# Key and query biases added in PSUM by a product, and elu+1 as one exponential and one min/max

## The chip, the cores and the metric

The kernel runs on one core of a Trainium2 chip. The metric is device time in microseconds (us), the median of several timed runs. A core has five engines that run side by side and wait for each other by semaphores: TensorE (PE in the rows; its weight loads are PEld), VectorE (DVE), ScalarE (ACT), GpSimd (POOL) and SyncE (SP, which here only issues transfers). TensorE writes its results into PSUM, a small memory of banks of 128 partitions x 512 fp32; VectorE and ScalarE read PSUM and SBUF, the main on-chip memory.

## The reference, cut to what matters

`x` and `ctx_1024` are (32, 128, 128): 32 sequences of 128 tokens of width 128. A layer of causal linear attention with 16 heads of width 8, then a layer of 8 experts of which each token takes two:

```
q  = layernorm(x) @ Wq + bq          # per token, 128 wide
k  = ctx @ Wk + bk
v  = ctx @ Wv + bv
qp = elu(q) + 1                      # = max(q + 1, min(exp(q), 1))
kp = elu(k) + 1
out[t] = sum over s <= t of (kp[s] . qp[t]) v[s]   per head
out    = (out / cumsum(qp)) @ Wo + bo
x = x + out
x = x + moe(layernorm(x))            # router, top 2 of 8, gated ffn
```

The biases are not zero: `bk` is drawn with a spread of 0.608, `bq` with 0.1.

## The kernel before, in words

The 32 sequences are worked in 8 units of 4 sequences, 512 tokens each. A unit's projections, scores and values are tiles of 128 partitions x 512. The code of every engine is written out by hand in the order in which it is to run, with waits on counting semaphores; `body(u, par)` of an engine is what it does while unit `u`'s attention runs. The units are overlapped: in `body(u)` the engines also do the *front* of unit `u + 1` (normalise, transpose and project x, project the context, elu+1, spread the keys and values) and the *tail* of unit `u - 1` (output projection, second layernorm, router, ranks). So `body(1)` to `body(6)` hold the fronts of units 2 to 7, and what precedes `body(0)` holds the front of unit 0.

The part that the change touches, in the front of unit `u + 1`:

- TensorE projects the keys into PSUM bank 1 (`front_project_k`, L1360), after VectorE has emptied the bank (`vexp_done`), and the queries into bank 0 (`front_project_q`, L1364), after ScalarE has copied the transposed x (`xT_copied`). The biases are not in these products.
- ScalarE computes elu+1's exponential in two steps: `front_neg` (L780) writes Relu(-(p + b)) from the bank p to `expn`, and `front_exp` (L785) overwrites it with Exp(-that), which is min(exp(p + b), 1). Index m is 0 for keys, 1 for queries.
- VectorE ends with one operation (`elu_k` L1000, `elu_q` L1004): max((p + (b + 1)), expn), the bank as its first tensor, b + 1 as a per-partition scalar.

In ScalarE's body the key's pair stands ahead of `front_norm` (L757, four operations, x normalised) and of `off_scores(u, 1)` (L817, scores copied from PSUM to `Pm`). VectorE's `mask_scores(u, 1)` (L1041) waits for that copy, and `front_z`, `weights` and `mask_scores(u, 2)` stand behind it. The query's Relu stands behind `off_scores(u, 2)`; then `tail_x2` (L822, the copy of the transposed second layernorm), and then the query's Exp.

TensorE's body holds the key projection ahead of `scores(u, 1)`, and the query projection between `scores(u, 2)` and the transposes of `tail_x2` (L1430). Products with a matrix of zeros (L1460) stand between them in the bodies 1 to 6.

The output bias and the router's bias are already added in PSUM in this way: GpSimd splits them into three bf16 parts that sum to the fp32 value (`biases`, L712 to L720, nine operations after `body(0)`'s own), puts these in rows 0, 32 and 64 of `bias_rows` with zeros between, and TensorE multiplies by a matrix of ones in bf16 (L1420, L1435), ahead of the fp32 products into the same bank.

After the attention a table of tiles is made and the experts run (L1552 to L1581). Its first tile waits until GpSimd has scattered the rows of units 0 to 5 to memory (L617, paced through the bodies, then without a pause) and SyncE has loaded the tile.

At the start SyncE issues the loads in a fixed order: x and context of unit 0, the weights Wk and Wq (`qk_pack`), Wv, Wo and others (`vo_pack`), three pieces of expert weights, then x and context of unit 1. VectorE takes the statistics of unit 1's x ahead of unit 0's `elu_k`.

Of the kernel before, what the change touches and what calls it, by code (L numbers as in the profile page):

```python
# [6 lines left out]
ALU = mybir.AluOpType  # L7
# [8 lines left out]
P = 128  # L16
# [5 lines left out]

def attention_moe_kernel(nc, x_tok, ctx_t, qk_pack, vo_pack, w_pack, out_tok):
    L, NB, D = x_tok.shape
# [3 lines left out]
    UB = 4  # L28
# [34 lines left out]
    with ExitStack() as ctx:  # L63
# [17 lines left out]
        carrier = sb("carrier", [P, 5])  # L81
        BIAS = P + 2 * E
# [4 lines left out]
        vo_s = sb("vo_s", [P, 4 * P + 3 * E])  # L87
        Wv_s, Wo_s, bv_b, _ = (vo_s[:, k * P:(k + 1) * P] for k in range(4))
        confT, _, wealth_b = (vo_s[:, 4 * P + k * E:4 * P + (k + 1) * E] for k in range(3))
        bq_neg, bk_neg = sb("bq_neg", [P, 1]), sb("bk_neg", [P, 1])  # L90
# [125 lines left out]
        exp_warm = sb("exp_warm", [P, 1])  # L216
        hid = sb("hid", [P, 2, HC * TT])
        hid_hi = sb("hid_hi", [P, 2, 2, HC * TT], F16)

# [39 lines left out]
        qk_loaded = sem("qk_loaded")  # L259
        const_loaded = sem("const_loaded")  # L260
        const_made = sem("const_made")
        const_dve = sem("const_dve")
# [101 lines left out]
        ROUTER = 8  # L364
        N_BIAS = 9
        N_EARLY = 13
        N_MADE = 35

# [72 lines left out]
        def _(sp):  # L441
# [23 lines left out]
            for m in range(3):  # L465
                load_w(0, m)
            load_x(1)
            load_ctx(1)
# [103 lines left out]
        def _(pool):  # L572
# [114 lines left out]
            made(pool.memset(seg_cols[:, E - 1:E], float(-(E - 1) * 3 * I)))  # L687
            made(pool.memset(cols_at[:, 0:1], 0))
            made(pool.memset(before[:], 0.0))
            made(pool.memset(unit_ids[:], TOP * UT))  # L690
# [11 lines left out]
            def biases():  # L702
# [10 lines left out]
                part(pool.tensor_copy(bias_part[0], given))  # L713
                part(pool.tensor_copy(bias_rows[0:1, :], bias_part[0][0:1, :]))
                part(pool.tensor_tensor(bias_rest, given, bias_part[0], ALU.subtract))
                part(pool.tensor_copy(bias_part[1], bias_rest))
# [32 lines left out]
        def _(act):  # L749
# [98 lines left out]
            def body(u, par):  # L848
# [115 lines left out]
        def _(dve):  # L964
# [33 lines left out]
            def elu_k(u, par):  # L998
                dve.wait_ge(exp_done, 2 * u + 1)
                dve.scalar_tensor_tensor(kT[:], bank[1][:], bk_one[:], expn[:, 0, :], ALU.add, ALU.max).then_inc(qk_done, 1)  # L1000

            def elu_q(u, par):
                dve.wait_ge(exp_done, 2 * u + 2)
                dve.scalar_tensor_tensor(qT[par][:], bank[0][:], bq_one[:], expn[:, 1, :], ALU.add, ALU.max).then_inc(qk_done, 1)  # L1004

# [340 lines left out]
        def _(pe):  # L1346
            def front_transpose_x(u):
# [17 lines left out]

# [49 lines left out]
            def tail_out(u):  # L1415
                if not first(u):
                    pe.wait_ge(rows_to_done, u)
                if first(u):
                    pe.wait_ge(bias_made, N_BIAS)
                pe.matmul(tail_bank(u).rearrange("p (b d) -> p b d", b=UB), ones_b[:], bias_rows[:, 0:P].unsqueeze(1).to_broadcast([P, UB, P]),  # L1420
                          start=True, stop=False, skip_group_check=True)
# [11 lines left out]
            def tail_logits(u):  # L1433
                pe.wait_ge(x2T_copied, u + 1)
                pe.matmul(tail_bank(u)[:, 0:UB * E].rearrange("p (b e) -> p b e", b=UB), ones_b[:], bias_rows[:, P + E:BIAS].unsqueeze(1).to_broadcast([P, UB, E]),  # L1435
                          start=True, stop=False, skip_group_check=True)
# [240 lines left out]
```

## Time and profile before

| | us |
|---|---|
| median of 3 timed runs | 344.05 |
| lowest and highest of them | 343.34, 345.0 |
| span of the profiled execution (first to last instruction) | 343.3 |
| TensorE busy | 296.6 (86%) |
| VectorE busy | 271.9 (79%) |
| ScalarE busy | 234.0 (68%) |
| GpSimd busy | 194.4 (57%) |

The profiled execution has no time of its own beside its span; the span lies 0.04 us below the lowest timed run and 0.75 us below the median. A busy share is an average over stages with different limits: the attention units and the experts' tiles each take about half of the span. To read a stage, look for the engine that never waits there, and for the one wait that it has.

### The profile page before, as it was taken

To read this page: it belongs to the slowest core of one execution; us is meant where nothing else is said; L and a number is where in the kernel's file an instruction comes from. 1 tells how busy PE (TensorE), PEld (TensorE's weight loads), DVE (VectorE), ACT (ScalarE), POOL (GpSimd) and SP (SyncE) were. 2 spreads that over 40 slices of the span, in tenths; PEclk is the share of its full clock that TensorE was granted. 3 is DMA by queue.
4 is the path that set the end of the run, shared out by engine and by line. 5 is a ranking of instruction groups with operands and counts; after the bars stand their busy time and mean duration, and the time that the engine had idled before them with its cause. 6 is when DMAs were issued, how large, how long until landed. Compare 5 with 4: busy or idle time off the path is not lost.

```text
span 343.3 us, 12426 instructions
## 1 busy us (share of the span) xinstructions
PE 296.6 (86%) x4520; PEld 241.5 (70%) x4520; DVE 271.9 (79%) x749; ACT 234.0 (68%) x480; POOL 194.4 (57%) x303
## 2 busy tenths in 40 slices
PE   7588888979888898978789989999999979799970
PEld 5367575746657575664568979989899969699930
DVE  6679898999999899999868697996678745567681
ACT  3587886959778795961747867767677756577720
POOL 6800306676677767587578757777455554245440
PEclk9789999999999999989989999999999999999996
DMA  7032322415233331320144314576799653432968
GB/s 246 18 94 63 95 63 60 128 33 143 77 103 104 100 103 34 84 90 33 35 91 87 73 41 75 149 127 181 232 202 256 198 156 41 70 71 63 290 185 301
DMA packets 50026, 39.45 MB, mean 115 GB/s; under 512 B 32806, under 2 KB 39340, under 8 KB 49968
## 3 DMA queue, kind: packets, MB, share of 16 engines
q1 hardware_dynamic: 44784, 28.63, 31.7%
q0 software_dynamic: 4320, 8.47, 8.7%
q10 hardware_dynamic: 864, 1.57, 1.2%
q8 instruction: 38, 0.62, 0.8%
q14 instruction: 20, 0.16, 0.2%
HBM read 15.16 MB, written 12.21 MB: 80 GB/s over the span
## 4 chain that ended last, share of the span: by engine, by line
PE 40%; DVE 28%; issue 9%; DMA 8%; ACT 7%; POOL 6%; SPq 1%; POOLq 0%; ACTq 0%; DVEq 0%
DVE Pm L1041 6%; PE bank L1552 4%; PE bank L1554 4%; PE bank L1553 4%; POOL by_expert L617 4%; PE scores L1554 4%; PE scores L1552 4%; PE scores L1553 4%; PE bank L1581 4%; PE bank L1573 4%; PE bank L1574 4%; DVE w_lo L1106 3%; DVE Vexp L1013 3%; PE bank L1360 3%; DMA xgT<-by_expert 2%
## 5 line engine op out<-in xcount | busy, mean ns | idle before, releaser
L617 POOL DMA_INDIRECT by_expert<-token_rows,rows_to x64 | 65.7, 1026 | 27.9 <-issue 18.9
L737 POOL DMA_INDIRECT by_token<-y_sb,row_meta x55 | 56.4, 1025 | 43.9 <-ACT y_sb L906 31.7
L1294 DVE SCALAR_TENSOR_TENSOR hid<-scores,silu 128x512 f32<-128x512 f32 x71 | 48.4, 690 | 34.6 <-PE scores L1554 29.2
L915 ACT ACTIVATE silu<-bank 128x512 f32<-128x512 f32 x71 | 42.0, 596 | 27.1 <-PE bank L1554 24.2
L922 ACT ACTIVATE hid_hi<-hid 128x512 f16<-128x512 f32 x71 | 44.4, 628 | 19.5 <-DVE hid L1294 18.5
L1300 DVE TENSOR_TENSOR Kexp<-hid,hid_hi 128x512 f16<-128x512 f32 x71 | 50.0, 715 | 9.0 <-ACT hid_hi L922 6.3
L1389 PEld LDWEIGHTS scores<-qT,Kexp 32*128 32x128 f32 x1024 | 33.1, 194 | 20.9 <-DVE Pm L1041 16.0
L1041 DVE TENSOR_TENSOR Pm<-scores,causal 128x512 f32<-128x512 f32 x64 | 41.1, 685 | 7.0 <-ACT Pm L817 6.5
L1389 PE MATMUL scores<-qT,Kexp 32*128 32x128 f32 (+1 forms) x1024 | 37.6, 285 | 9.9 <-DVE Pm L1041 6.7
L817 ACT ACTIVATE Pm<-scores 128x512 f32<-128x512 f32 x32 | 18.8, 588 | 24.3 <-PE scores L1389 24.2
L1574 PE MATMUL bank<-w_lo,hid_hi 128*128 x248 | 34.3, 219 | 0.0
L1573 PE MATMUL bank<-w_hi,hid_hi 128*128 x248 | 34.3, 219 | 0.0
L1405 PE MATMUL bank<-Pm,Vexp 128*32 128x64 f32 (+1 forms) x1024 | 27.9, 250 | 7.2 <-DVE Pm L1041 7.2
L1552 PE MATMUL bank<-xgT,w_hi 128*128 128x256 f16 x96 | 26.7, 278 | 4.5 <-DMA xgT<-by_expert 2.5
L1405 PEld LDWEIGHTS bank<-Pm,Vexp 128*32 128x32 f32 x1024 | 22.7, 110 | 11.1 <-DVE Pm L1041 8.1
L1554 PE MATMUL bank<-xgT,w_lo 128*128 128x256 f16 x96 | 26.7, 278 | 0.0
L1553 PE MATMUL bank<-xgT,w_hi 128*128 128x256 f16 x96 | 26.6, 277 | 0.0
L1552 PE MATMUL scores<-xgT,w_hi 128*128 128x256 f16 x96 | 26.5, 276 | 0.0
L584 POOL TENSOR_TENSOR nm<-zero,mv 128x4 f32<-128x4 f32 x16 | 3.2, 202 | 41.1 <-DVE mv L971 41.0
L1553 PE MATMUL scores<-xgT,w_hi 128*128 128x256 f16 x96 | 26.5, 276 | 0.0
L1554 PE MATMUL scores<-xgT,w_lo 128*128 128x256 f16 x96 | 26.5, 276 | 0.0
L1574 PEld LDWEIGHTS bank<-w_lo,hid_hi 128*128 128x128 f16 x248 | 24.3, 98 | 0.3
(392 smaller groups left out, 793.5 us busy)
## 6 DMA issues: line engine op xcount, KB each, us to landing
w_raw<-in_w_pack_dram SPq DMA_DIRECT2D x24, 256.0 KB, 3.0
x_all<-in_x_tok_dram SPq DMA_DIRECT2D x8, 256.0 KB, 3.3
cT<-in_ctx_t_dram SPq DMA_DIRECT2D x8, 256.0 KB, 3.0
out_dram<-x_all ACTq DMA_DIRECT2D x6, 256.0 KB, 5.0
by_expert<-pad_row SPq DMA_DIRECT2D x9, 130.0 KB
by_expert<-token_rows,rows_to POOLq DMA_INDIRECT x64
token_rows<-by_token SPq DMA_DIRECT2D x2, 512.0 KB, 4.8
by_token<-y_sb,row_meta POOLq DMA_INDIRECT x55
```

The lines of the kernel that those rows point to most:

```text
L617: pool.indirect_dma_start(by_expert, bass.IndirectOffsetOnAxis(ap=rows_to[u % 2][:, s, b:b + 1], axis=0), token_rows[u % 2][:, b, s, :], N ...
L737: pool.indirect_dma_start(by_token, bass.IndirectOffsetOnAxis(ap=number, axis=0), y_sb[:, k, s, :], None, bounds_check=NT * TOP - 1, oob_i ...
L1041: dve.tensor_tensor(Pm[:, b % 2, :, at:at + CH].rearrange("p (r j) t -> p r j t", r=RG), score_groups[:, :, :, at:at + CH], causal[:].unsq ...
L1294: dve.scalar_tensor_tensor(hid[:, slot, :], bank[2 + slot], 1.0 / WSCALE, silu[:, slot, :], ALU.mult, ALU.mult).then_inc(hid_done, 1)
L1300: dve.tensor_tensor(hid_lo[:, k % 2, slot, :], hid[:, slot, :], hid_hi[:, k % 2, slot, :], ALU.subtract).then_inc(lo_done, 1)
L1389: ins = pe.matmul(scores4[:, r, j * SPAN + at:j * SPAN + at + n], Kexp[par][rows, c, 2 * j:2 * j + 2, :], qT[par][rows, c * CH:c * CH + n] ...
L1405: ins = pe.matmul(bank[6][32 * r:32 * r + 32, c * CH:c * CH + n], Vexp[par][:, c, 2 * r:2 * r + 2, :].rearrange("p g k -> p (g k)")[:, 16 ...
L1552: pe.matmul(ps, high, x_hi, start=(c == 0), stop=False, skip_group_check=True)
L1553: pe.matmul(ps, high, x_lo, start=False, stop=False, skip_group_check=True)
L1554: ins = pe.matmul(ps, low, x_hi, start=False, stop=True, skip_group_check=True)
L1573: pe.matmul(ps, hid_hi[:, k % 2, slot, h], high, start=(c == 0 and s == 0), stop=False, skip_group_check=True)
L1574: pe.matmul(ps, hid_hi[:, k % 2, slot, h], low, start=False, stop=False, skip_group_check=True)
```

## The change: what it does

From unit 2 on (`PLAIN = 2`) a bf16 product, `lift`, writes b + 1 into the bank ahead of the projection, which then accumulates on it: the bank holds p + b + 1. ScalarE's exponential reads the bank itself, Exp(bank - 1) with the -1 from a one-column tile `minus_one`, and there is no Relu. VectorE's operation becomes max(min(expn, 1), bank): the bank is now its second tensor, and its scalar is the constant 1. Units 0 and 1 keep the old form.

For this the key and query biases go, raised by 1, through the same split as the other two: `bias_rows` grows from 144 to 392 columns and GpSimd's work on it from nine operations to ten. The biases come in a transfer of their own, `bias_pack`, that lands in `hid` (the experts' tile, unused by then); `vo_pack` loses the columns that held the two old ones.

```
@@ sync
             for m in range(3):
                 load_w(0, m)
+            sp.dma_start(bias_given, bias_pack).then_inc(bias_loaded, 16)
             load_x(1)
             load_ctx(1)
@@ gpsimd
+            made(pool.memset(minus_one[:], -1.0))
...
-                pool.wait_ge(const_loaded, 16)
-                given = vo_s[:, 3 * P:3 * P + BIAS]
+                pool.wait_ge(bias_loaded, 16)
+                lifted = bias_given[:, 0:QK].rearrange("p (m d) -> p m d", m=2)
+                part(pool.tensor_tensor(lifted, lifted, ones[:].unsqueeze(1).to_broadcast([P, 2, P]), ALU.add))
                 part(pool.memset(bias_rows[:], 0.0))
@@ scalar
-                act.wait_ge(neg_done, 2 * u + m + 1)
-                act.activation(expn[:, m, :], expn[:, m, :], ACT.Exp, scale=-1.0).then_inc(exp_done, 1)
+                if u < PLAIN:
+                    act.wait_ge(neg_done, 2 * u + m + 1)
+                    act.activation(expn[:, m, :], expn[:, m, :], ACT.Exp, scale=-1.0).then_inc(exp_done, 1)
+                else:
+                    if u == PLAIN:
+                        act.wait_ge(const_made, N_MADE)
+                    ps, ready = ((bank[1], k_ps), (bank[0], q_ps))[m]
+                    act.wait_ge(ready, u + 1)
+                    act.activation(expn[:, m, :], ps[:], ACT.Exp, bias=minus_one[:]).then_inc(exp_done, 1)
...
-                    front_neg(u + 1, 0)
+                    if u + 1 < PLAIN:
+                        front_neg(u + 1, 0)
                     front_exp(u + 1, 0)
                     front_norm(u + 1)
...
-                if not last(u):
+                if u + 1 < PLAIN:
                     front_neg(u + 1, 1)
@@ vector, from unit 2 on (elu_q likewise with bank[0] and qT)
-                dve.scalar_tensor_tensor(kT[:], bank[1][:], bk_one[:], expn[:, 0, :], ALU.add, ALU.max).then_inc(qk_done, 1)
+                    dve.scalar_tensor_tensor(kT[:], expn[:, 0, :], 1.0, bank[1][:], ALU.min, ALU.max).then_inc(qk_done, 1)
@@ tensor
+            def lift(ps, m):
+                pe.wait_ge(bias_made, N_BIAS)
+                pe.matmul(ps.rearrange("p (b t) -> p b t", b=UB), bias_rows[:, m * P:(m + 1) * P], ones_b[:].unsqueeze(1).to_broadcast([P, UB, P]),
+                          start=True, stop=False, skip_group_check=True)
...
+                if u >= PLAIN:
+                    lift(bank[1], 0)
-                pe.matmul(bank[1], Wk_s, cT[par][:], start=True, stop=True).then_inc(k_ps, 1)
+                pe.matmul(bank[1], Wk_s, cT[par][:], start=(u < PLAIN), stop=True, skip_group_check=True).then_inc(k_ps, 1)
...
                 pe.wait_ge(xT_copied, u + 1)
-                pe.matmul(bank[0], Wq_s, xT[:], start=True, stop=True).then_inc(q_ps, 1)
+                if u >= PLAIN:
+                    lift(bank[0], 1)
+                pe.matmul(bank[0], Wq_s, xT[:], start=(u < PLAIN), stop=True, skip_group_check=True).then_inc(q_ps, 1)
```

How this stands in the engines' queues, at the places where another engine waits. A row is one instruction, or several alike, with its line in its own kernel, what it writes and reads, and the semaphores that it waits for. First ScalarE in the body of a unit from 2 on, from the last copy of the expert weights (`w_hi`) to the scores' copy for which VectorE waits. Before:

```order
L753 ACTIVATE w_hi<-w_raw 128x512 [waits w_loaded0_2]
L780 ACTIVATE expn<-bank,bk_neg 128x512 [waits k_ps]
L785 ACTIVATE expn<-expn 128x512 [waits neg_done]
L757 ACTIVATE xhat<-x_all,shift,rstd 128x128 [waits xT_ps,shift1_done]
L757 ACTIVATE xhat<-x_all,shift,rstd 128x128 x3
L817 ACTIVATE Pm<-scores 128x8x64 [waits av_done,scores_ps]
```

Now:

```order
L761 ACTIVATE w_hi<-w_raw 128x512 [waits w_loaded0_2]
L800 ACTIVATE expn<-bank,minus_one 128x512 [waits k_ps]
L765 ACTIVATE xhat<-x_all,shift,rstd 128x128 [waits xT_ps,shift1_done]
L765 ACTIVATE xhat<-x_all,shift,rstd 128x128 x3
L832 ACTIVATE Pm<-scores 128x8x64 [waits av_done,scores_ps]
```

The Relu is gone, and the exponential that stood behind it waits for the key projection itself (`k_ps`).

ScalarE again, later in the same body, from the second layernorm (`x2hat`) and the third copy of scores to the query's exponential. Before:

```order
L757 ACTIVATE x2hat<-x_all,shift,rstd 128x128 x3
L817 ACTIVATE Pm<-scores 128x8x64 [waits av_done,scores_ps]
L780 ACTIVATE expn<-bank,bq_neg 128x512 [waits q_ps]
L822 ACTIVATE x2T<-bank 128x512 [waits x2T_ps]
L785 ACTIVATE expn<-expn 128x512 [waits neg_done]
```

Now:

```order
L765 ACTIVATE x2hat<-x_all,shift,rstd 128x128 x3
L832 ACTIVATE Pm<-scores 128x8x64 [waits av_done,scores_ps]
L837 ACTIVATE x2T<-bank 128x512 [waits x2T_ps]
L800 ACTIVATE expn<-bank,minus_one 128x512 [waits q_ps]
L818 ACTIVATE zinv<-Z,seed_bias 128x512 [waits rz_done,z_done]
```

The query's Relu is gone from between the copy of scores and the copy of the transposed layernorm (`x2T`), and the exponential keeps its place behind that copy.

TensorE around the key projection of `body(1)`, behind the zero products. Before:

```order
L1460 MATMUL bank<-ones_b,zero_b 128x512 x4
L1360 MATMUL bank<-cT,qk_s 128x512 [waits vexp_done]
L1389 MATMUL scores<-qT,Kexp 128x128 [waits diag_done]
L1389 MATMUL scores<-qT,Kexp 128x128 x3
L1389 MATMUL scores<-qT,Kexp 128x64 x4
```

Now:

```order
L1492 MATMUL bank<-ones_b,zero_b 128x512 x4
L1380 MATMUL bank<-ones_b,bias_rows 128x512 [waits bias_made,vexp_done]
L1390 MATMUL bank<-cT,qk_s 128x512
L1421 MATMUL scores<-qT,Kexp 128x128 [waits diag_done]
L1421 MATMUL scores<-qT,Kexp 128x128 x3
L1421 MATMUL scores<-qT,Kexp 128x64 x4
```

The bias product takes over the wait for VectorE's emptying of the bank and stands, with a wait on GpSimd's bias work, ahead of the projection.

SyncE at the start, from the load of `vo_pack` to that of unit 1's context. Before:

```order
L464 DMA vo_s<-in_vo_pack_dram 128x536
L459 DMA w_raw<-in_w_pack_dram 128x512 x3
L446 DMA x_all<-in_x_tok_dram 128x512
L453 DMA cT<-in_ctx_t_dram 128x512
L453 DMA cT<-in_ctx_t_dram 128x512 [waits k_ps,v_ps]
```

Now:

```order
L469 DMA vo_s<-in_vo_pack_dram 128x400
L464 DMA w_raw<-in_w_pack_dram 128x512 x3
L472 DMA hid<-in_bias_pack_dram 128x392
L451 DMA x_all<-in_x_tok_dram 128x512
L458 DMA cT<-in_ctx_t_dram 128x512
L458 DMA cT<-in_ctx_t_dram 128x512 [waits k_ps,v_ps]
```

The bias load stands ahead of unit 1's x and context, and the load of `vo_s` is 136 columns narrower.

## Rows read from the trace of the kernel before

**Rows 1.** Top line of the page: the span of the profiled execution.

```profile
span 343.3 us, 12426 instructions
```

**Rows 2.** Waits of VectorE, 34 to 150 us: total us, times, longest us.

```profile
DVE Pm L1041 <- ACT Pm L817: 4.4, 6, 0.7
```

**Rows 3.** Chain of waits, unit 4: start us, duration us, engine, tile, line.

```profile
94.94 1.14 PE bank L1360 x2
96.10 0.70 ACT expn L780
```

**Rows 4.** ScalarE, unit 4: start, busy us, engine, line, operation, tiles, shapes, count.

```profile
96.82 0.63 ACT L785 ACTIVATE expn<-expn 128x512 f32<-128x512 f32 x1
97.36 1.63 ACT L757 ACTIVATE xhat<-x_all,shift,rstd 128x128 f32<-128x128 f32 x4
103.10 0.68 ACT L780 ACTIVATE expn<-bank,bq_neg 128x512 f32<-128x512 f32 x1
103.67 0.59 ACT L822 ACTIVATE x2T<-bank 128x512 f32<-128x512 f32 x1
104.15 0.63 ACT L785 ACTIVATE expn<-expn 128x512 f32<-128x512 f32 x1
```

**Rows 5.** VectorE, unit 4; in brackets the idle us before and its releaser.

```profile
98.05 0.72 DVE L1000 SCALAR_TENSOR_TENSOR kT<-bank,bk_one,expn 128x512 f32<-128x512 f32 x1
99.51 1.29 DVE L1041 TENSOR_TENSOR Pm<-scores,causal 128x512 f32<-128x512 f32 x2 [0.74 <-ACT Pm L817]
104.97 0.74 DVE L1004 SCALAR_TENSOR_TENSOR qT<-bank,bq_one,expn 128x512 f32<-128x512 f32 x1
```

**Rows 6.** Bias products: TensorE timeline, chain, then weight loads (PEld).

```profile
32.85 0.39 PE L1420 MATMUL bank<-bias_rows,ones_b 128*128 128x512 bf16 x1
...
177.74 0.22 PE scores L1420
...
91.84 0.10 PEld L1420 LDWEIGHTS bank<-bias_rows,ones_b 128*128 128x128 bf16 x1 [0.28 <-DVE rows_to L1100]
94.94 0.30 PEld L1360 LDWEIGHTS bank<-cT,qk_s 128*128 128x128 f32 x2 [0.97 <-DVE Vexp L1013]
```

**Rows 7.** TensorE, unit 4: query projection and the transposes behind it.

```profile
101.90 1.12 PE L1364 MATMUL bank<-xT,qk_s 128*128 128x512 f32 x2
102.86 0.60 PE L1430 MATMUL bank<-ident,x2hat 128*128 128x128 f32 x4
```

**Rows 8.** Page, costliest groups: busy us, mean ns, idle before.

```profile
L1294 DVE SCALAR_TENSOR_TENSOR hid<-scores,silu 128x512 f32<-128x512 f32 x71 | 48.4, 690 | 34.6 <-PE scores L1554 29.2
```

**Rows 9.** Chain, start; then a window: engines busy, PEclk, DMA share, GB/s.

```profile
4.08 5.90 DMA x_all<-in_x_tok_dram
...
7.50:8.00 0.50, 0.50 (x20) 0.50 (x22) 0.50 (x1) 0.50 (x2) 0.43 (x2) 1.00 1.02 385
```

**Rows 10.** GpSimd's bias work, first and last of nine; VectorE's first scans.

```profile
14.12 0.22 POOL L712 MEMSET bias_rows<- 128x144 bf16 x1
17.31 0.30 POOL L720 COPY bias_rows<-xgT 1x144 bf16<-1x144 bf16 x1
...
23.43 1.36 DVE L1021 TENSOR_TENSOR_SCAN Z<-ones,qT 128x128 f32<-128x128 f32 x4
```

**Rows 11.** One VectorE line twice; GpSimd beside the second.

```profile
149.71 0.71 DVE L1034 SCALAR_TENSOR_TENSOR Z<-zser_oT,zinv 128x512 f32<-128x512 f32 x1
...
170.98 1.68 DVE L1034 SCALAR_TENSOR_TENSOR Z<-zser_oT,zinv 128x512 f32<-128x512 f32 x1
...
170.95 2.72 POOL L603 TENSOR_TENSOR token_rows<-x2hat,token_rows 128x512 f16<-128x512 f32 x2 [3.12 <-ACT token_rows L829]
```

**Rows 12.** GpSimd in unit 6; chain at the first expert tile's load.

```profile
143.09 1.21 POOL L617 DMA_INDIRECT by_expert<-token_rows,rows_to  x1 [1.86 <-ACT Pm L817]
...
170.35 2.81 DMA xgT<-by_expert
```

**Rows 13.** Window, start of the experts' stage; PEclk stands third from the right.

```profile
175.00:176.00 1.00, 1.00 (x7) 0.69 (x6) 0.12 (x1) 0.12 (x1) 0.89 (x1) 0.50 0.31 30
```

More of the change, by code:

```diff
@@ L20, with attention_moe_kernel @@
 SEED_BIAS = -129.0 * math.log(2.0) - 0.0299
-def attention_moe_kernel(nc, x_tok, ctx_t, qk_pack, vo_pack, w_pack, out_tok):
+def attention_moe_kernel(nc, x_tok, ctx_t, qk_pack, vo_pack, bias_pack, w_pack, out_tok):
     L, NB, D = x_tok.shape
@@ L81, in attention_moe_kernel @@
         carrier = sb("carrier", [P, 5])
-        BIAS = P + 2 * E
+        QK = 2 * P
+        BIAS = QK + P + E
         bias_rows = sb("bias_rows", [P, BIAS], BF16)
@@ L86, in attention_moe_kernel @@
         Wk_s, Wq_s, bk_c, bq_c = qk_s[:, 0:P], qk_s[:, P:2 * P], qk_s[:, 2 * P:2 * P + 1], qk_s[:, 2 * P + 1:2 * P + 2]
-        vo_s = sb("vo_s", [P, 4 * P + 3 * E])
-        Wv_s, Wo_s, bv_b, _ = (vo_s[:, k * P:(k + 1) * P] for k in range(4))
-        confT, _, wealth_b = (vo_s[:, 4 * P + k * E:4 * P + (k + 1) * E] for k in range(3))
+        vo_s = sb("vo_s", [P, 3 * P + 2 * E])
+        Wv_s, Wo_s, bv_b = (vo_s[:, k * P:(k + 1) * P] for k in range(3))
+        confT, wealth_b = (vo_s[:, 3 * P + k * E:3 * P + (k + 1) * E] for k in range(2))
+        minus_one = sb("minus_one", [P, 1])
         bq_neg, bk_neg = sb("bq_neg", [P, 1]), sb("bk_neg", [P, 1])
@@ L217, in attention_moe_kernel @@
         hid = sb("hid", [P, 2, HC * TT])
+        bias_given = hid[:, 0, 0:BIAS]
         hid_hi = sb("hid_hi", [P, 2, 2, HC * TT], F16)
@@ L260, in attention_moe_kernel @@
         const_loaded = sem("const_loaded")
+        bias_loaded = sem("bias_loaded")
         const_made = sem("const_made")
@@ L364, in attention_moe_kernel @@
         ROUTER = 8
-        N_BIAS = 9
+        N_BIAS = 10
+        PLAIN = 2
         N_EARLY = 13
-        N_MADE = 35
+        N_MADE = 36
         def units(engine, body):
@@ L999, in elu_k @@
                 dve.wait_ge(exp_done, 2 * u + 1)
-                dve.scalar_tensor_tensor(kT[:], bank[1][:], bk_one[:], expn[:, 0, :], ALU.add, ALU.max).then_inc(qk_done, 1)
+                if u < PLAIN:
+                    dve.scalar_tensor_tensor(kT[:], bank[1][:], bk_one[:], expn[:, 0, :], ALU.add, ALU.max).then_inc(qk_done, 1)
+                else:
+                    dve.scalar_tensor_tensor(kT[:], expn[:, 0, :], 1.0, bank[1][:], ALU.min, ALU.max).then_inc(qk_done, 1)
             def elu_q(u, par):
                 dve.wait_ge(exp_done, 2 * u + 2)
-                dve.scalar_tensor_tensor(qT[par][:], bank[0][:], bq_one[:], expn[:, 1, :], ALU.add, ALU.max).then_inc(qk_done, 1)
+                if u < PLAIN:
+                    dve.scalar_tensor_tensor(qT[par][:], bank[0][:], bq_one[:], expn[:, 1, :], ALU.add, ALU.max).then_inc(qk_done, 1)
+                else:
+                    dve.scalar_tensor_tensor(qT[par][:], expn[:, 1, :], 1.0, bank[0][:], ALU.min, ALU.max).then_inc(qk_done, 1)
             def front_v(u, par):
@@ L1419, in tail_out @@
                     pe.wait_ge(bias_made, N_BIAS)
-                pe.matmul(tail_bank(u).rearrange("p (b d) -> p b d", b=UB), ones_b[:], bias_rows[:, 0:P].unsqueeze(1).to_broadcast([P, UB, P]),
+                pe.matmul(tail_bank(u).rearrange("p (b d) -> p b d", b=UB), ones_b[:], bias_rows[:, QK:QK + P].unsqueeze(1).to_broadcast([P, UB, P]),
                           start=True, stop=False, skip_group_check=True)
@@ L1434, in tail_logits @@
                 pe.wait_ge(x2T_copied, u + 1)
-                pe.matmul(tail_bank(u)[:, 0:UB * E].rearrange("p (b e) -> p b e", b=UB), ones_b[:], bias_rows[:, P + E:BIAS].unsqueeze(1).to_broadcast([P, UB, E]),
+                pe.matmul(tail_bank(u)[:, 0:UB * E].rearrange("p (b e) -> p b e", b=UB), ones_b[:], bias_rows[:, QK + P:BIAS].unsqueeze(1).to_broadcast([P, UB, E]),
                           start=True, stop=False, skip_group_check=True)
@@ L1661 @@
         "qk_pack": _np.concatenate([g["L0_xattn_Wk"], g["L0_xattn_Wq"], g["L0_xattn_bk"][:, None], g["L0_xattn_bq"][:, None]], axis=1),
-        "vo_pack": _np.concatenate([g["L0_xattn_Wv"][:, by_half], g["L0_xattn_Wo"], rows("L0_xattn_bv")[:, by_half], rows("L0_xattn_bo"),
-                                    g["L0_ffn_conf_w"].T, rows("L0_ffn_conf_b"), rows("L0_ffn_wealth")], axis=1),
+        "vo_pack": _np.concatenate([g["L0_xattn_Wv"][:, by_half], g["L0_xattn_Wo"], rows("L0_xattn_bv")[:, by_half],
+                                    g["L0_ffn_conf_w"].T, rows("L0_ffn_wealth")], axis=1),
+        "bias_pack": _np.concatenate([rows("L0_xattn_bk"), rows("L0_xattn_bq"), rows("L0_xattn_bo"), rows("L0_ffn_conf_b")], axis=1),
         "w_pack": _np.concatenate([g["L0_ffn_gate_w"].transpose(0, 2, 1), g["L0_ffn_up_w"].transpose(0, 2, 1),
```

4 lines of the change are left out of this document (2 added, 2 removed).

## The prediction

> **What bounds the kernel now.** The page's top line gives the time against which the sum is made: a span of 343.3 us [rows 1], 0.75 below the median of the runs shown. The page names no time of this execution beside its span, and the lowest run stands at 343.34, so nothing that counts lies around it. I read three views, in this order. First VectorE's waits over the bodies 1 to 6, 34 to 150 us, where the changed units are. The reader is to see how short the list is: one entry, 4.4 us in 6 times, at most 0.7 each, and it names ScalarE's copy of scores to Pm [rows 2]. VectorE is what bounds these bodies, and whatever makes ScalarE or TensorE faster there can win no more than this wait. Second the chain of waits in unit 4, since the wait's cause is not the copy itself: the chain leaves VectorE for the key projection on TensorE, goes on to the Relu [rows 3] and returns to VectorE through the copy. Third ScalarE's and VectorE's timelines around it: Relu at 96.10, exponential at 96.82, four normalisations from 97.36, then the copy; VectorE ends the key's elu at 98.05 + 0.72 = 98.77 and stands idle for 0.74 until 99.51 [rows 3 to 5]. So the key's Relu lies on the path; the other five bodies repeat this.
>
> **The key's half, per body.** Relu to exponential is a step of 96.82 - 96.10 = 0.72, and it goes. The exponential stays, but reads PSUM and takes its -1 through a pointer. The trace has no such exponential. Before, it took 0.63 and its successor began 97.36 - 96.82 = 0.54 later; the query's Relu, with the same source, size and a pointer bias, takes 0.68 with its successor 103.67 - 103.10 = 0.57 later [rows 4]. I take the nearer row and charge 0.03, so ScalarE gives 0.69. The lowest charge is below nothing: the copy from PSUM without a pointer takes 0.59, with a successor 0.48 later [rows 4], so -0.06; the highest is 0.1, the whole spread of the three durations.
>
> The same row can be weighed with the Trainium skill, "ScalarE: Activation LUTs", section "What ACT_TABLE_LOAD costs": each pointer operand adds about 93 ns to an activation. The 0.68 against 0.59 of the two PSUM readers agrees with it. By the rule alone the charge would be 0.09 and the final saving about 2.3 instead of 2.66; the trace's exponential without a pointer, at 0.63, shows that its old SBUF source was the dearer one, and that is why I stay at 0.03.
>
> Against it stands the lift, behind the wait for the bank and ahead of the projection, with nothing beside it. A bf16 product of the same size takes 0.22 of the chain just ahead of fp32 products (177.74), and 0.39 counted whole (32.85) [rows 6]. From below: its weights load in 0.10, and the load of Wk, 0.30 for two and so 0.15 each, then runs beside it [rows 6], which leaves 0.22 + 0.10 - 0.15 = 0.17; nothing excludes that, and nothing speaks for less. I take 0.22, the row in the same position. Its wait for GpSimd's bias work is met long before (below).
>
> Net 0.69 - 0.22 = 0.47 a body. The copy's end and the mask move from 99.51 to 99.04, still behind the key's elu at 98.77, so VectorE goes on waiting for 0.27 and the whole 0.47 counts. Six bodies: 2.82.
>
> **The query's half.** Here I expect nothing from the Relu. VectorE starts the query's elu at 104.97 straight behind its own work [rows 5]; only being late matters. With the Relu gone, ScalarE comes to the x2T copy 0.57 sooner, at 103.10 instead of 103.67. But TensorE's projection (101.90) now has the lift ahead of it, so the transposes move from 102.86 to 103.08 and end 0.60 later, at 103.68 [rows 7]. The copy therefore begins at about 103.70, as before; the exponential 0.48 behind it, at 104.18, and with 0.68 it ends at 104.86. That is 0.11 ahead of VectorE. The Relu's place is taken by a wait for the transposes, and the cover of the edit is this 0.11: with a lift of 0.39 the exponential ends at 105.03 and VectorE waits 0.06 or a little more in each body. (All of these are in the body's own frame, which the key's half moves as a whole.)
>
> **VectorE's own operation.** It loses its scalar pointer and takes the bank as second tensor. The nearest row with a constant, one PSUM tensor and one SBUF tensor is 690 ns [rows 8] against 0.72 and 0.74 [rows 5]. The key's has 0.27 of room, so only the query's counts: 6 x 0.03 = 0.18. No row has PSUM in second place; the ends are this gain and a second pass over the elements, 0.69 more, taken up as a rival.
>
> **The start.** The chain at the start goes through the load of unit 1's x, issued at 4.08 and landed 5.90 later [rows 9], because its statistics stand ahead of unit 0's elu. The bias load is issued ahead of it. It brings 392 columns, `vo_pack` loses 136: 256 columns of 128 fp32 rows, 131 kB more in the line before that x. The engines are saturated then, at 385 GB/s [rows 9]: 0.34. Nothing hides it, VectorE has no other work there. From below 0, if the pieces of several loads are interleaved so that the smaller `vo_pack` makes up for it; from above 0.85, with the issue of one more transfer on top (unit 1's x is the eighth, issued at 4.08, so 4.08 / 8 = 0.51 at most for one). I take 0.34.
>
> GpSimd's bias work ran from 14.12 to 17.61, nine operations at 144 columns [rows 10]. If all of it grows with the columns, 3.49 x 392 / 144 = 9.5, with 0.7 for the tenth operation it ends at 24.3; some of each operation is fixed, so sooner. The first product that needs it ran at 32.85 [rows 6]: hidden by 8 us. The memset of minus_one, in the same queue, is hidden by the same.
>
> **The sum.** 2.82 + 0.18 - 0.34 = 2.66 off the span of 343.3. It carries to the end: GpSimd's scatter in unit 6 waited for ScalarE's copy, idle for 1.86 before [rows 12], and from there it runs on to the load of the first expert tile at 170.35, so that load moves with the copy; behind it the experts' stage is unchanged. Taken off the median: 344.05 - 2.66 = 341.4.
>
> **Rivals.** *The gain is eaten on TensorE (no change).* The lift costs its whole 0.39, the key's half leaves 0.69 - 0.39 = 0.30, the query's exponential comes 0.06 to 0.1 late, which leaves 0.22: six bodies 1.3, less a start of 0.85, 343.6. For it: the lift is serial in both places and the query has only 0.11 of room. Against: the chain's 0.22.
>
> *PSUM in second place costs a second pass (slower).* The place is VectorE's two elu operations, the price up to 0.69 each. The query's counts in full; the key's then ends at 99.46, and the mask comes at 99.48, so the key's half wins 0.03. Per body -0.66, in all 6 x 0.66 + 0.34 = 4.3 slower: 348.4. It decides from a price x at which x + (x - 0.27) = 0.47, x = 0.37. For it only that no row shows the form; against it that with the bank in first place the 512 elements take one pass.
>
> *GpSimd's longer bias work meets VectorE's scans.* Early rows of unit 0's sums stand at 23.43 [rows 10], 0.34 later now, and my latest end of the bias work is 24.3. One VectorE line with two SBUF tensors took 0.71 alone and 1.68 while GpSimd worked on 512 columns [rows 11], 0.97 more; one such meeting gives 342.4. Against it: the fixed share of each GpSimd operation ends the work sooner than 23.8. The Trainium skill, "SBUF — State Buffer", section "SBUF: two separate sides", has the rule: a VectorE operation with two SBUF inputs and a GpSimd operation that reads SBUF exclude each other for a whole instruction. The 1.68 agrees.
>
> *The change does less than it says* can be left aside: the Relu stays for units 0 and 1 alone, as the order shows, and their bodies are not in the sum.
>
> **How the numbers follow.** Forecast 0.63: its own range is 339.5 to 342.4. The lower end is VectorE's whole wait, 4.4, with the elu's 0.18 and no loss at the start; the upper a lift halfway to 0.39 and a start of 0.85. It holds one thing more: the first expert products run in a window of granted clock 0.50, 1.2 of 2.4 GHz [rows 13], after a wait for their tile, and each microsecond by which that window grows or shrinks is worth half a microsecond. TensorE eats it: 0.22. GpSimd meets the scans: 0.07. Second pass: 0.08. Range 339.8 to 344.0. A measurement of this kernel can tell about 0.5%, 1.7 us, from no change: faster than 342.3 is nearly all of the forecast and half of the scans' case, 0.64; within it 0.27; slower 0.09.
>
> **What would show it.** In the profile after, VectorE's wait for the Pm copy falls from 0.7 to about 0.3 in six bodies; the step from the key projection's end to the first normalisation falls by 0.7; the exponential takes 0.66 to 0.70; ScalarE waits about half a microsecond for the transposes ahead of x2T; unit 1's x lands near 10.3. I am wrong if VectorE shows a new wait for the exponential ahead of the query's elu, if its elu takes 1.2 or more, if the body gets shorter by less than 0.3, or if what the bodies save is gone again when the first expert tile is loaded.

## The result, and the profile after

| | before | changed |
|---|---|---|
| median of 20 timed runs each, us | 344.6 | 342.94 |
| lowest and highest, us | 343.19, 347.31 | 339.69, 345.07 |
| ratio, 95% interval | | 0.9925 [0.9904, 0.9946] |
| span of the profiled execution, us | 343.3 | 338.0 |

The change gains 0.75%, that is 2.6 us (344.6 x 0.0075; 1.9 to 3.3 by the interval). The ratio leaves out three runs of the changed kernel that count as slow, 344.9 to 345.07; by the medians of all runs, as the table has them, the gain is 1.66. The forecast was 2.66 off a median of 344.05. The two profiles differ by 5.3, twice as much: the profiled execution after took 339.7 us, one of the shortest, so its total isn't to be read as the gain.

The top line of the page after, against [rows 1]:

```profile
span 338.0 us, 12455 instructions
```

VectorE's waits, 33 to 148 us (us in total, times, longest), against [rows 2]. The wait for the Pm copy falls from 4.4 to 1.6, from 0.7 to 0.3 at most (the list has one more row, 0.9 once, in the last body):

```profile
DVE Pm L1063 <- ACT Pm L832: 1.6, 6, 0.3
```

Of ScalarE's own waits in the same stretch one row is new: ScalarE now stands before the x2T copy until TensorE's transposes are there, 0.4 in each body.

```profile
ACT x2T L837 <- PE bank L1462: 2.5, 6, 0.4
```

ScalarE in unit 4, against [rows 4]:

```profile
93.06 0.69 ACT L800 ACTIVATE expn<-bank,minus_one 128x512 f32<-128x512 f32 x1 [2.34 <-PE bank L1390]
93.65 1.64 ACT L765 ACTIVATE xhat<-x_all,shift,rstd 128x128 f32<-128x128 f32 x4
95.19 0.57 ACT L832 ACTIVATE Pm<-scores 128x512 f32<-128x512 f32 x1
...
99.91 0.60 ACT L837 ACTIVATE x2T<-bank 128x512 f32<-128x512 f32 x1 [0.42 <-PE bank L1462]
100.41 0.68 ACT L800 ACTIVATE expn<-bank,minus_one 128x512 f32<-128x512 f32 x1
```

The Relu is gone; the exponential, now from PSUM and with a pointer, has its successor 93.65 - 93.06 = 0.59 later. VectorE in unit 4, against [rows 5]:

```profile
94.88 0.65 DVE L1019 SCALAR_TENSOR_TENSOR kT<-expn,bank 128x512 f32<-128x512 f32 x1
95.80 1.29 DVE L1063 TENSOR_TENSOR Pm<-scores,causal 128x512 f32<-128x512 f32 x2 [0.26 <-ACT Pm L832]
...
101.27 0.67 DVE L1026 SCALAR_TENSOR_TENSOR qT<-expn,bank 128x512 f32<-128x512 f32 x1
```

The elu operations take 0.65 and 0.67 instead of 0.72 and 0.74, and the idle time ahead of the mask 0.26 instead of 0.74. No wait stands ahead of the query's elu. TensorE in unit 4, then its weight loads, against [rows 3, 6, 7]:

```profile
91.78 0.39 PE L1380 MATMUL bank<-ones_b,bias_rows 128*128 128x512 bf16 x1 [0.48 <-DVE Vexp L1035]
92.00 1.02 PE L1390 MATMUL bank<-cT,qk_s 128*128 128x512 f32 x2
...
98.19 0.39 PE L1380 MATMUL bank<-ones_b,bias_rows 128*128 128x512 bf16 x1
98.42 1.02 PE L1396 MATMUL bank<-xT,qk_s 128*128 128x512 f32 x2
99.28 0.60 PE L1462 MATMUL bank<-ident,x2hat 128*128 128x128 f32 x4
```

```profile
91.77 0.10 PEld L1380 LDWEIGHTS bank<-ones_b,bias_rows 128*128 128x128 bf16 x1 [0.97 <-DVE Vexp L1035]
91.78 0.42 PEld L1390 LDWEIGHTS bank<-cT,qk_s 128*128 128x128 f32 x2
```

From the lift's start to the exponential's start it is 93.06 - 91.78 = 1.28; before, from the projection's start to the Relu's, 1.16 [rows 3]. The lift costs 0.12, because the projection itself takes 1.02 instead of 1.12 [rows 7]: the first of its two weight loads runs beside the lift (the second row of the weight loads). The body's step, first scan of one unit to first scan of the next, is 19.79 before (mean of the five between units 1 and 6) and 19.18 after.

GpSimd's bias work, first and last row after, then its scatter of unit 6, against [rows 10, 12]:

```profile
14.52 0.73 POOL L719 TENSOR_TENSOR hid<-hid,ones 128x256 f32<-128x256 f32 x1
...
20.70 0.51 POOL L728 COPY bias_rows<-xgT 1x392 bf16<-1x392 bf16 x1
...
138.17 1.22 POOL L623 DMA_INDIRECT by_expert<-token_rows,rows_to  x1 [1.19 <-ACT Pm L832]
```

VectorE's first scan, and the chain at the start, against [rows 9, 10]:

```profile
22.06 1.36 DVE L1043 TENSOR_TENSOR_SCAN Z<-ones,qT 128x128 f32<-128x128 f32 x4
```

```profile
4.56 5.01 DMA x_all<-in_x_tok_dram
```

The bias work ends at 21.2, ahead of the scans. Unit 1's x lands at 9.57, not at 10.3.

### The profile page after: what moved, and what is told of

It reads as the page before. It is cut to its first block, busy times and chain, and to the rows that moved or that the text cites. A ratio compares the mean times of both kernels' runs of the same rounds, so it can differ in the third digit from the quotient of the medians.

```text
span 338.0 us, 12455 instructions
## 1 busy us (share of the span) xinstructions
PE 297.2 (88%) x4532; PEld 243.6 (72%) x4532; DVE 270.6 (80%) x749; ACT 227.9 (67%) x468; POOL 198.9 (59%) x305
## 4 chain that ended last, share of the span: by engine, by line
PE 39%; DVE 35%; issue 9%; ACT 7%; DMA 4%; POOL 4%; SPq 1%; POOLq 0%; ACTq 0%; DVEq 0%
DVE Pm L1063 7%; PE bank L1584 4%; DVE w_lo L1128 4%; PE scores L1586 4%; PE scores L1584 4%; PE bank L1586 4%; PE scores L1585 4%; PE bank L1585 4%; PE bank L1613 4%; PE bank L1605 4%; PE bank L1606 4%; ACT xhat L765 3%; DVE Vexp L1035 3%; DVE Z L1043 3%; PE bank L1390 2%
## 5 line engine op out<-in xcount | busy, mean ns | idle before, releaser
L938 ACT ACTIVATE hid_hi<-hid 128x512 f16<-128x512 f32 x71 | 44.4, 628 | 19.2 <-DVE hid L1316 17.7
L1606 PEld LDWEIGHTS bank<-w_lo,hid_hi 128*128 128x128 f16 x248 | 24.3, 98 | 0.3
L1605 PEld LDWEIGHTS bank<-w_hi,hid_hi 128*128 128x128 f16 x248 | 24.2, 98 | 0.3
```

Of the source, the lines that this page charges most:

```text
L1605: pe.matmul(ps, hid_hi[:, k % 2, slot, h], high, start=(c == 0 and s == 0), stop=False, skip_group_check=True)
L1606: pe.matmul(ps, hid_hi[:, k % 2, slot, h], low, start=False, stop=False, skip_group_check=True)
```

## The experiments

Each kernel ran in five rounds; the ratio is to the kernel before on the same chip. The columns behind the ratio come from one profile each: the body's step as above, the start of the first expert product, and the rest, which is the span minus that start.

| kernel | ratio, 95% | body step | first expert product | rest |
|---|---|---|---|---|
| before | 1 | 19.79 | 173.28 | 170.02 |
| changed | 0.9925 [0.9904, 0.9946] | 19.18 | 168.35 | 169.65 |
| changed again | 0.9923 [0.9886, 0.9959] | 19.17 | 169.48 | 172.02 |
| bias load last | 0.9917 [0.9880, 0.9955] | 19.17 | 168.16 | 172.24 |
| normalise first | 0.9900 [0.9850, 0.9950] | 18.91 | 167.78 | 171.62 |
| both of these | 0.9866 [0.9815, 0.9918] | 18.91 | 168.36 | 170.34 |
| key alone | 0.9889 [0.9846, 0.9932] | 19.26 | 169.38 | 170.62 |
| query alone | 0.9999 [0.9968, 1.0030] | 19.74 | 172.69 | 169.41 |
| before, normalise first | 0.9952 [0.9918, 0.9986] | 19.39 | 170.56 | 169.44 |
| a second lift | 1.0011 [0.9979, 1.0043] | 19.41 | 171.88 | 171.82 |
| changed, last weights late | 0.9878 [0.9829, 0.9926] | 19.17 | 169.43 | 169.47 |
| before, last weights late | 0.9965 [0.9934, 0.9997] | 19.81 | 173.15 | 168.45 |
| all three edits | 0.9798 [0.9753, 0.9843] | 18.92 | 168.02 | 168.78 |

**The changed kernel again**, no edit.

> The changed kernel once more, for a second look at where its time goes. Theory (the key's chain): the step between the second mask operations of consecutive bodies is 19.17 us against 19.79 before, so six bodies give 3.7 us; VectorE's wait for the Pm copy is 0.26 a body. The start is late by 0.34 with respect to before, so the time is about 3.3 us below before. Rival (the start is what the single trace showed): unit 1's x lands at 9.6 and body 0 is 1.3 shorter than before in this trace too, 5 us below before.

Median 342.45. The body's step and VectorE's wait repeat to 0.01; the first expert product comes 3.8 earlier than before instead of 4.9, since unit 0's first scan came at 22.99 instead of 22.06, although unit 1's x was early again (its statistics at 9.70). The traces' clock records show why: TensorE's granted clock was 0.50, the lower of its two levels (1.2 of 2.4 GHz), from 14.3 to 17.7 us in the first profile, but from 13.1 to 19.9 here and from 13.2 to 20.0 before; unit 0's scores and values took 1.58 and 1.27 on the chain there, 1.99 and 1.93 here. So about 1 us of the 1.37 by which that scan came earlier in the first profile than in the kernel before is the clock's, not the change's. The time is 2.65 below (344.56 x 0.0077; 1.4 to 3.9 by the interval), which leaves the expected 3.3 in and the rival's 5 out. What repeats is the bodies: from unit 0's first scan to unit 7's 137.39 before, 133.86 after, 133.77 here, so 3.5 to 3.6 us saved.

**The bias load last.**

```
-            sp.dma_start(bias_given, bias_pack).then_inc(bias_loaded, 16)
             load_x(1)
             load_ctx(1)
+            sp.dma_start(bias_given, bias_pack).then_inc(bias_loaded, 16)
```

> The bias load is issued behind unit 1's x and context. Theory (131 kB in the line ahead of that x cost 0.34): x lands 0.3 to 0.8 us earlier than in the changed kernel, and the whole is faster by the same 0.3 to 0.8. Rival (loads are interleaved, the place in the line does not matter): landing and time as in the changed kernel, within 0.2.

Unit 1's statistics start at 9.46, against 9.73 and 9.70 in the two profiles of the changed kernel, and the bodies are unchanged; 0.24 to 0.27 is a little under the expected 0.3. The time, 342.04 against 342.45, differs by less than its interval, 1.3 us to either side, so a gain of a few tenths is not shown by the time.

**Normalise first**: in ScalarE's body the four normalisations ahead of the key's exponential.

```
+                    front_norm(u + 1)
                     if u + 1 < PLAIN:
                         front_neg(u + 1, 0)
                     front_exp(u + 1, 0)
-                    front_norm(u + 1)
```

> In each body from 0 to 6 ScalarE's four normalisations stand ahead of the key's exponential, whose projection they need not wait for. Theory (the remaining 0.26 of VectorE's wait lies on the chain projection, exponential, normalisations, copy): the normalisations run beside the projection, the wait for the Pm copy falls from 0.26 to 0.05 or less, the body from 19.17 to 18.9, six bodies 1.5 us faster than the changed kernel. Rival (the copy waits for the scores on TensorE, or VectorE then waits for the exponential): the wait stays at 0.2 or more under another name and the time does not move.

The step falls to 18.91 and VectorE's list of waits from 33 to 148 us is empty. ScalarE in unit 4:

```profile
92.46 1.65 ACT L765 ACTIVATE xhat<-x_all,shift,rstd 128x128 f32<-128x128 f32 x4 [1.54 <-POOL shift L595]
94.02 0.67 ACT L800 ACTIVATE expn<-bank,minus_one 128x512 f32<-128x512 f32 x1
94.58 0.58 ACT L832 ACTIVATE Pm<-scores 128x512 f32<-128x512 f32 x1
```

The normalisations now run in the time in which ScalarE waited for the key projection (2.34 in the changed kernel). So the rest of the wait was ScalarE's order, and with it gone VectorE alone sets the body. In time the ratio falls by 0.0023 against the changed kernel on the same chip, 0.8 us where 1.5 was expected; both intervals are wider than that.

**Both of these.**

> Both edits together, the normalisations ahead of the exponential and the bias load last. Theory: they do not touch each other, so 1.5 plus 0.3 to 0.8, about 2 us faster than the changed kernel. Rival: only the larger of the two shows.

Median 340.6. It is faster than the kernel before, and its interval lies below most of the changed kernel's. By the ratios it is 0.0057 faster than the changed kernel on the same chip, 2.0 us, as expected; but normalise first alone (0.9900) lies within its interval, so that the second edit adds to the first is not shown.

**The key alone**: the query keeps Relu, Exp and its scalar; no lift into bank 0. TensorE's part of the edit:

```
-                if u >= PLAIN:
-                    lift(bank[0], 1)
-                pe.matmul(bank[0], Wq_s, xT[:], start=(u < PLAIN), stop=True, ...)
+                pe.matmul(bank[0], Wq_s, xT[:], start=True, stop=True, ...)
```

> Only the key has the new form from unit 2 on; the query keeps Relu, exponential and pointer scalar. Theory (the gain is the key's chain): a body of 19.79 - 0.55 = 19.24, VectorE's wait for the Pm copy 0.26, 3.3 us in six bodies; the missing 0.07 is the query's elu with its pointer. Rival (what counts is ScalarE's load, and each of the two Relus is worth half): a body of about 19.48.

**The query alone**: the mirror of it.

```
-                if u >= PLAIN:
-                    lift(bank[1], 0)
-                pe.matmul(bank[1], Wk_s, cT[par][:], start=(u < PLAIN), stop=True, ...)
+                pe.matmul(bank[1], Wk_s, cT[par][:], start=True, stop=True, ...)
```

> Only the query has the new form from unit 2 on; the key keeps the old one. Theory: the query's Relu turns into a wait of ScalarE for the transposes, so a body of 19.79 - 0.07 = 19.72, the 0.07 from VectorE's elu without a pointer, VectorE's wait for the Pm copy still 0.74, ScalarE's wait ahead of the x2T copy 0.4; with the start's 0.34 the time is that of before. Rival (ScalarE's load counts): a body of about 19.48 and 1.5 us below before.

VectorE's waits, 33 to 148 us, of the key alone and then of the query alone:

```profile
DVE Pm L1063 <- ACT Pm L832: 1.6, 6, 0.3
```

```profile
DVE Pm L1062 <- ACT Pm L832: 4.4, 6, 0.7
```

The key's half takes the whole of the wait that goes, and 0.53 of the step; the query's takes 0.05, about what its elu is shorter by. The two add up to 0.58 of the 0.61. In time the query alone is no change, the key alone at least as good as both.

**The kernel before, normalise first**: the same swap as above, `front_norm` ahead of `front_neg` and `front_exp`.

> The kernel before, with the four normalisations ahead of the key's Relu and exponential and nothing else. Theory (the Relu was on the path only because the normalisations stood behind it): VectorE's wait for the Pm copy goes from 0.74 to 0 or nearly, in its place it waits up to 0.35 for the key's exponential, and the body goes from 19.79 to about 19.35, 2.6 us in six bodies, with the Relu still there. Rival (the Relu and the exponential are on the path wherever they stand): a body of 19.7 or more.

VectorE's waits, 33 to 148 us:

```profile
DVE kT L1000 <- ACT expn L785: 1.5, 6, 0.3
```

An order of three calls, with no arithmetic changed, saves 0.40 of the body's step, two thirds of what the change saves. The copy is no longer late; the key's exponential is, by 0.3. The time falls by 1.7 us (344.9 x 0.0048; 0.5 to 2.8 by the interval), where 2.6 was expected.

**A second lift**: a bf16 product with zeros behind the key's lift.

```
                     lift(bank[1], 0)
+                    pe.matmul(bank[1]..., zero_b[:], ones_b..., start=False, stop=False, ...)
```

> The changed kernel with a second product of the lift's size, of zeros, between the key's lift and its projection; the sum in the bank is the same. Theory (the lift is serial and on the path, its first one cost 0.12 only because the weights of Wk load beside it): the whole of a second one counts, 0.21 a body, VectorE's wait from 0.26 to 0.47, 1.3 us slower than the changed kernel. Rival (the lift hides behind the mask that the scores wait for): wait and body unchanged.

VectorE's waits, 33 to 148 us, then TensorE in unit 4:

```profile
DVE Pm L1063 <- ACT Pm L832: 2.9, 6, 0.5
```

```profile
93.57 0.39 PE L1380 MATMUL bank<-ones_b,bias_rows 128*128 128x512 bf16 x1 [0.48 <-DVE Vexp L1035]
93.80 0.38 PE L1390 MATMUL bank<-ones_b,zero_b 128*128 128x512 bf16 x1
94.01 1.02 PE L1392 MATMUL bank<-cT,qk_s 128*128 128x512 f32 x2
```

The second product costs 94.01 - 93.80 = 0.21 on the path, and the step grows by 0.23: a product in a row is what the prediction priced, 0.22. The first behind the wait costs 0.12. The step was foreseen; the time, 345.04, is about 3 us above the changed kernel's although the six bodies explain 1.4. The rest is not explained; the granted clock, 0.968 as the mean of its timed runs against 0.969 in the changed kernel's, does not do it either.

**The last weights late.** Two things did not fit by now: the bodies save 3.5, the time 2.6, and the experts' stage is longer in most kernels with the key's new form. TensorE at the second single tile (of one block of rows; the tiles before have two), about 275 us, after:

```profile
275.12 0.22 PE L1584 MATMUL bank<-xgT,w_raw 128*128 128x128 f16 x1 [2.52 <-issue]
```

and before, at the second and the third:

```profile
278.47 0.22 PE L1552 MATMUL bank<-xgT,w_raw 128*128 128x128 f16 x1 [0.84 <-issue]
...
282.13 0.22 PE L1552 MATMUL bank<-xgT,Pm 128*128 128x128 f16 x1 [1.49 <-issue]
```

SyncE's issues after show what was ahead of that tile's load (269.86): 768 kB of weights, the two `single_more` rows, that TensorE first uses at 319.3.

```profile
265.42 1.30 SPq L526 DMA_TRANSPOSE xgT<-by_expert  x1
266.93 0.40 SPq L527 DMA_DIRECT2D row_meta<-by_expert  x1
268.50 0.53 SPq L538 DMA_DIRECT2D single_more<-w_hi  x1
269.14 0.52 SPq L539 DMA_DIRECT2D single_more<-w_lo  x1
269.86 1.24 SPq L526 DMA_TRANSPOSE xgT<-by_expert  x1
```

The edit, in the changed kernel and in the kernel before:

```
-                if 0 <= i - SINGLE_AT < SINGLES:
+                if 0 <= i - SINGLE_AT < SINGLES - 2:
                     load_single(i - SINGLE_AT)
             for j in range(LASTS):
                 load_last(j)
+            for j in (SINGLES - 2, SINGLES - 1):
+                load_single(j)
```

> The changed kernel; SyncE issues the loads of the last two single tiles' weights (two of 384 kB each) behind the loads of all tiles instead of between the loads of tiles 23 to 25. They are used some 50 us later, so nothing else has to move. The six bodies save 3.7 us but the time falls by 2.6; in the changed kernel TensorE waits 2.5 to 2.8 us at the start of the second single tile (before: 0.84), for nothing that the profile names. Theory (that tile's load is late: SyncE's row of loads has its own pace there, and the tile's load queues behind these weights): the wait falls below 1 us, TensorE's next wait (about 292 us) may stay, and the time falls by another 1.5 to 2.5 us, to about 340.4, ratio to the kernel before 0.988. Rival (TensorE waits for something of its own, its instructions or a semaphore of another engine): the wait stays at 2.5 and the time at 342.4, ratio 0.9925.

> The kernel before with the same move of the last two single tiles' weight loads. Its own waits at the second and third single tile are 0.84 and 1.49 us. Theory of the late load: both fall below 0.5 and the time by 1 to 2 us, to about 343.1, ratio 0.996; the difference between this kernel and the changed one with the same move is then the whole gain of the bodies and the start, 3.7 to 4 us, that is a ratio of about 0.989 between the two. Rival: 344.6, ratio 1.0, and a difference between the two of 2.6 us (0.9925).

SyncE's issues of tiles 24 and 25 in the changed kernel with the edit, then TensorE where the wait was:

```profile
263.34 1.18 SPq L526 DMA_TRANSPOSE xgT<-by_expert  x1
264.72 0.42 SPq L527 DMA_DIRECT2D row_meta<-by_expert  x1
265.33 1.18 SPq L526 DMA_TRANSPOSE xgT<-by_expert  x1
```

```profile
274.96 0.39 PE L1615 MATMUL bank<-w_hi,Kexp 128*128 x4
275.19 0.22 PE L1586 MATMUL bank<-xgT,w_raw 128*128 128x128 f16 x1
```

The tile is asked for 4.5 earlier and the wait is gone, in both kernels; of TensorE's waits from 262 to 300 us only the one of 1.8 stays, at 289.7 and 293.2. That TensorE waited for this load is shown. Its sequencer, which issues its instructions, waits ahead of each tile for `hid_done` and the tile's load. How long, from 255 to 300 us (ns: least, median, longest), in the changed kernel without and with the edit:

```profile
L1579 PEldq EVENT_SEMAPHORE  x14: 51/51/3611, 256.9 to 299.8; - x14
```

```profile
L1581 PEldq EVENT_SEMAPHORE  x15: 51/51/51, 255.7 to 299.9; - x15
```

And in the traces' semaphore events the last part of the tile lands 0.09 ahead of the product in each of the ten profiles without the edit (275.03 after, 278.38 before); `hid_done` had come by 272.06 and 277.09. The issue was not the late part: it stood 2.74 us ahead of the time at which TensorE was ready after, 2.30 before. The load itself was long, 5.17 us after and 3.05 before. It took 4.4 to 5.2 in the six profiles with both halves of the change and 3.05 to 3.5 in the other four, all with the same weights ahead of it, and 3.2 to 3.6 with the edit. So the weights in the queue are not enough to make it long, and why it is long with both halves stays open; the edit helps the kernel before by the earlier issue alone.

Medians 340.62 and 343.62: by the ratios the move is worth 1.6 us in the changed kernel ((0.9925 - 0.9878) x 344.6), where the two intervals overlap, and 1.2 in the kernel before, whose interval ends just below 1. What of the bodies' gain the late load took back, 1.6 - 1.2 = 0.4, is smaller than the intervals. With the edit in both the gain is 0.9878 / 0.9965 = 0.991, 3.0 us; the two intervals together leave 1 to 5. The expected 3.7 lies within, as 2.6 does.

**All three edits**: normalise first, the bias load last, the last weights late.

> The changed kernel with the normalisations ahead of the exponential, the biases' load last, and the last two single tiles' weights late. Theory: the gain of the first two (ratio 0.987) and of the third add up: about 338.6, ratio 0.982; body step 18.9. Rival (the wait is not for the load): 340.2, ratio 0.987.

Median 337.99, 0.9798 [0.9753, 0.9843] of the kernel before: the best version, and within the interval the gains add up.

## Why the prediction was right, step by step

**What bounds the bodies.** Right. VectorE's wait was the whole of what could be won; a kernel without it (normalise first) has a step of 18.91, and there no wait of VectorE is left. That is 0.88 less than before: the wait's 0.74, and 0.07 from each of the two elu operations.

**The key's half, 0.47 a body.** Right in mechanism, and a little short. The Relu's 0.72 went. The exponential's charge was 0.59 - 0.54 = 0.05, not 0.03. The Trainium skill, "ScalarE: Activation LUTs", section "What ACT_TABLE_LOAD costs", would charge 93 ns for the pointer: 0.68 against the 0.59 of the copies from PSUM agrees with it. But against the old exponential, which read SBUF and took 0.63 [rows 4], the charge is the 0.05 measured, and the sum goes by that. The lift was mis-sized: 0.12 in place of 0.22, below even my lower bound of 0.17. That bound charged the lift's own weight load, 0.10, in full; but the load is recorded beside the lift (91.77 and 91.78), and the projection starts 92.00 - 91.78 = 0.22 behind the lift all the same. What is won back is 0.10 of the projection, whose first weights load beside the lift. So 0.72 - 0.05 - 0.12 = 0.55 a body, and the key alone shows 0.53 in the step.

**VectorE's wait, 0.74 to 0.27.** It went to 0.26. The better lift (0.10 a body) does not show there, because the key's elu became 0.07 shorter as well and moved VectorE's own end ahead by it.

**The query's half.** Right: nothing from the Relu, which became a wait of 0.42 for the transposes where about half a microsecond was said. The exponential ends at 100.41 + 0.68 = 101.09, 0.18 ahead of VectorE at 101.27. The margin held.

**VectorE's own operation.** Right in sign, and mis-sized: 0.07 less instead of 0.03, both for the key and the query. PSUM as second tensor is no dearer, so the rival of a second pass is dead.

**The start, 0.34 lost.** Wrong. Unit 1's x landed at 9.57 instead of near 10.3, and its statistics began earlier than before. Over the profiles they began at 10.11 to 10.21 with the load order of before (three kernels), at 9.53 to 10.76 with the bias load ahead (seven) and at 9.46 to 9.89 with it last (three). The load's place is worth about 0.26 by the means of the last two, 9.92 and 9.66, less than the spread; but the step that counted 131 kB more as a later landing against the kernel before fails. Why that x is earlier in most of them I can't say.

**GpSimd.** Right. Its bias work ended at 21.2, sooner than my latest end of 24.3, and met no scan.

**The sum and its carrying.** That 2.66 lies so near the measured 2.6 is luck: the terms offset each other. The bodies saved 3.5 to 3.6 instead of 3.0 (five steps of 0.61, and 0.49 in the first). The first expert product took it over in full: 173.28 to 168.35 is the bodies' 3.53 and the 1.37 by which unit 0's first scan came earlier in that profile, most of it the clock's. Behind it the experts' stage was not unchanged, as I had said: TensorE is earlier there, SyncE's loads have a pace of their own, and waits for them vary from none to 3.1 us between profiles with the same order of loads. They are one place where a part of the gain goes; the 0.4 measured is half of the 0.9 that is missing, and neither is sure.

The granted clock is the other place, and the prediction had named it, at half a microsecond for each at 0.50. TensorE behind the second single tile (275.95 and 275.12), from 276 to 278 us, in the changed kernel's second profile and in its first; the granted clock is third from the right:

```profile
276.00:278.00 2.00, 2.00 (x20) 2.00 (x21) 0.00 (x0) 0.58 (x1) 0.85 (x1) 0.50 0.45 98
```

```profile
276.00:278.00 2.00, 2.00 (x40) 2.00 (x37) 0.69 (x1) 1.15 (x3) 0.31 (x1) 1.00 0.30 71
```

At 0.50 half as many products run. From the first expert product to the last, less TensorE's waits, the thirteen profiles took 146 us where none of it ran at 0.50 (three of them), 147.6 with 3.4 us at 0.50 (before), 147.4 with 2.9 (after) and 150.7 with 10.2 (changed again): each microsecond at 0.50 costs 0.47. With the waits that is why the last column of the table moves by up to 2.8 us without any edit in that stage. The timed runs had a mean granted clock of 0.9716 to 0.9725 in the kernel before (its three series beside the experiments) and of 0.9686 and 0.9687 in the changed kernel's two. The difference, 0.0035 of 341 us, is 2.4 us more at 0.50, and at 0.47 each 1.1 us: an estimate, but as much as the 0.9. No edit tested the clock by itself, so where the 0.9 went stays open between the two.

One more step was wrong without touching the sum: nothing was said to lie around the span. In the runs with both numbers the time is mostly 1.7 above the span (339.7 for 338.0 after), so the profiled execution before [rows 1] took about 345.0, the longest of the three runs, and not less than their median.

**Rivals.** TensorE did not eat the gain: its price was 0.12, not 0.39. GpSimd met nothing. The change did what it says.

## What to carry to other kernels

Before taking an operation off a waiting engine's path, look at what stands ahead of the waited operation in its engine's order and does not depend on the same thing: moving the normalisations ahead of the key's two steps saved 0.40 a body without the change, where the change saved 0.61, and 0.27 more on top of it. A product put ahead of another at the end of a wait cost less here than one in a row (0.12 against 0.21), since the next product's weights load beside it. A gain in one stage can move the next stage's engine against loads with a pace of their own, so look there for loads that stand ahead of what is needed first, and compare the granted clock before a difference between two profiles is put down to the edit.

## What the runs showed of the hardware that was not expected

- A VectorE scalar_tensor_tensor of 128x512 fp32 took 0.65 to 0.67 with a constant scalar and PSUM as second tensor, 0.72 to 0.74 with a pointer and PSUM as first. Which of the two differences does it is not separated.
- With 131 kB more ahead of it in SyncE's order, a load landed at 9.57 instead of 9.98; over seven profiles with that order the statistics that wait for it began between 9.53 and 10.76.
- The load of the second single tile took 3.05 us in one kernel and 5.17 in another, with the same 768 kB of weights issued in the 1.4 us before it, and 3.2 to 3.6 with none. The Trainium skill, "DMA: Bandwidth & Descriptors", section "Queues, rings and completion order", says that each DMA engine takes up the descriptors of a ring in their order. A long load behind the weights would agree with it, but the short one stood behind them as well, so no run here shows it.
- In three of the six profiles with a wait of 1.6 to 3.1 us at that tile TensorE's granted clock fell to 0.50 within 1.1 us of the wait's end (changed again at 275.9, normalise first at 275.6, a second lift at 279.3); in the other three it did not fall there.
